# A recurrent layer's time loop: value and beta from one selection product, temporaries in PSUM, 64 steps a turn

## The reference, cut to what matters

```python
def step(S, inp):
    ...
    kn = k_t / (jnp.linalg.norm(k_t, axis=-1, keepdims=True) + 1e-06)
    retrieved = jnp.einsum('bnij,bnj->bni', S, kn)
    delta = v_t - retrieved
    outer = delta[..., :, None] * kn[..., None, :]
    S_upd = jnp.tanh(beta_t[..., None] * S + outer)
    S_new = (1.0 - w) * S + w * S_upd
    Sq = jnp.einsum('bnij,bj->bni', S_new, q_t)
```

## Time and profile before

| | us |
|---|---|
| median of three runs | 9550.41 |
| lowest and highest of them | 9549.36, 9557.72 |
| the profiled execution | 9542.88 |
| its span, first to last instruction | 9541.1 |
| TensorE matmul busy | 7287.1 (76%) |
| TensorE weight loads busy | 4453.7 (47%) |
| VectorE busy | 6764.2 (71%) |
| ScalarE busy | 3257.0 (34%) |
| POOL busy | 3224.7 (34%) |
| mean granted TensorE clock | 0.853 |

### The profile page before, as it was taken

The page is one execution under the profiler, slowest core; times in us unless marked ns, Lnnn a source line. Parts: engine busy times, 40 slices in busy tenths (PEclk is TensorE's granted clock), DMA queues, the critical chain, the costliest instruction groups (busy, mean ns, idle before and its releaser), DMA issues. The chain is left out here.

```text
span 9541.1 us, 245537 instructions
## 1 busy us (share of the span) xinstructions
PE 7287.1 (76%) x92569; PEld 4453.7 (47%) x92569; DVE 6764.2 (71%) x15000; ACT 3257.0 (34%) x5970; POOL 3224.7 (34%) x3982
## 2 busy tenths in 40 slices
PE   4888888888874826656845768888888888888887
PEld 3666666666621212223223345545455545454554
DVE  7777777777758475765485557777777777777776
ACT  2222222222243313223413334444444444444444
POOL 1333333333300000210040035555555555555553
PEclk7888888888887867656865779999999999999999
DMA  0000000000000000000000031111111111111111
GB/s 18 1 1 1 1 1 1 1 1 1 1 5 1 15 0 0 0 0 1 0 0 1 1 120 54 53 53 54 48 56 51 54 51 51 56 51 56 51 56 57
DMA packets 156976, 243.21 MB, mean 25 GB/s; under 512 B 21617, under 2 KB 136849, under 8 KB 150161
## 3 DMA queue, kind: packets, MB, share of 16 engines
q1 hardware_dynamic: 155920, 228.84, 7.8%
HBM read 187.06 MB, written 13.66 MB: 21 GB/s over the span
## 5 line engine op out<-in xcount | busy, mean ns | idle before, releaser
L2751 POOL TENSOR_TENSOR big<-big 128x512 f32<-128x512 f32 x776 | 1040.1, 1373 | 278.4 <-DMA big<-norms 270.7
L2741 POOL TENSOR_TENSOR big<-big 128x512 f32<-128x512 f32 x388 | 494.7, 1275 | 1819.8 <-DVE big L2583 1819.8
L882 POOL TENSOR_TENSOR big<-big 128x128 f32<-128x128 f32 x1024 | 518.3, 506 | 1569.7 <-DVE big L820 1567.4
L604 ACT ACTIVATE big<-big 128x128 f32<-128x128 f32 x1024 | 316.8, 309 | 1902.0 <-DVE big L778 1876.8
L1856 POOL TENSOR_TENSOR small<-big 128x480 f32<-128x480 f32 (+14 forms) x240 | 220.9, 954 | 2187.2 <-ACT big L1614 1866.5
L2158 PE MATMUL banks<-hidden,big 128*128 128x256 f32 x3104 | 828.9, 401 | 111.8 <-DVE big L2583 41.1
L514 PE MATMUL banks<-big,constants_on_chip 128*128 128x128 f32 x2048 | 533.3, 347 | 409.8 <-DVE big L811 408.2
L337 PE MATMUL banks<-big,constants_on_chip 128*128 128x512 f32 (+15 forms) x1088 | 533.5, 644 | 355.2 <-DVE big L1747 191.3
L337 PE MATMUL banks<-big,weights_even 128*128 128x512 f32 (+5 forms) x1152 | 620.5, 692 | 235.0 <-DVE big L1137 45.1
L2222 PE MATMUL banks<-big,hidden 128*32 128x512 f32 x6144 | 770.5, 600 | 4.1 <-ACT big L2473 4.1
L2201 PEld LDWEIGHTS banks<-big 32*32 32x32 f32 x49152 | 535.2, 103 | 471.8 <-issue 471.1
(11 more groups left out here) (349 smaller groups left out, 15896.3 us busy)
## 6 DMA issues: line engine op xcount, KB each, us to landing
big<-norms SPq DMA_DIRECT2D x776, 128.0 KB, 2.9
big<-qk SPq DMA_DIRECT2D x50, 512.0 KB, 4.8
big<-vo SPq DMA_DIRECT2D x25, 1024.0 KB, 5.8
weights_odd<-ffn SPq DMA_DIRECT2D x25, 537.5 KB, 4.6
hidden<-big SPq DMA_DIRECT2D x171, 64.0 KB, 12.9
hidden<-big SPq DMA_DIRECT2D x25, 256.0 KB, 3.8
hidden<-big SPq DMA_DIRECT2D x25, 255.8 KB, 4.0
big<-pairs SPq DMA_DIRECT2D x6, 1024.0 KB, 10.4
```

Of the source, the lines that this page charges most:

```text
L882: nc.gpsimd.tensor_tensor(full(u["kS"][s % 2]), full(S), by(u["ko_c"]), ALU.mult).then_inc(*e.did(("kS", s)))
L2741: self.nc.gpsimd.tensor_tensor(dst, cos, sin, ALU.add).then_inc(*e.did(("turned_pair", f, name, g)))
L2751: self.nc.gpsimd.tensor_tensor(x, x, u["norms"][:, n, g].unsqueeze(1).broadcast_to([P, 2, QTOK]), ALU.mult).then_inc(*e.did(("scaled", f, ...
```

## The change

- A turn holds 64 steps in place of 32, so there are 16 turns.
- Ahead of the loop v and beta of all tokens are computed (`all_tokens`: 128 products of 32 rows by 128 columns each for v and for beta) and kept in SBUF. `xrep`, `repeat_x`, `values`, `logits` and the sigmoids of the loop are gone, and `knext`, the shifted copy of the keys, too.
- In the loop one product per step, `value_and_beta`, takes v(s) and beta(s) out of a 128 x 256 tile of 32 steps (`vb`) with a selection matrix (`own`, the identity repeated); v lands in columns 0 to 127 and beta in columns 128 to 255 of the step's bank (banks 0 and 1 in turn).
- outer and wT are in PSUM bank 2, arg and T in bank 3. bS reads beta from the step's bank.
- TensorE waits for bS(s) ahead of the kS product of delta(s), besides kS and kT; VectorE waits for v(s+1) ahead of bS.
- The small copies for the next 32 steps, and the copies of v and beta, are on ScalarE behind the tanh; VectorE keeps two small instructions per half turn.
- The bf16 product that nobody reads stays, and writes bank 5.

```diff
-STEPS = 32
-PARTS = 1
+STEPS = 64
...
+        own=b[6].rearrange("p (s c) -> p s c", c=P),
...
+        step_bank=core.bank[0:2], outer=core.bank[2][:, 0:128], wT=core.bank[2][:, 128:256],
+        arg=core.bank[3][:, 0:128], T=core.bank[3][:, 128:256], out_bank=[core.bank[4], core.bank[7]],
...
+    def all_tokens(bank, weight, g, start):
+
+        for m in range(4):
+            for b in range(BATCH):
+                at = b * SEQ + (4 * g + m) * HALF_STEPS
+                mm = nc.tensor.matmul(bank[32 * b:32 * b + 32, m * P:(m + 1) * P], u["xp"][:, at:at + HALF_STEPS], weight,
+                                      start=start, stop=True, skip_group_check=True)
+        return mm
...
+    def value_and_beta(s, label):
+
+        nc.tensor.matmul(u["step_bank"][s % 2][:, 0:2 * P], u["own"][:, s % HALF_STEPS, :], u["vb"][s // HALF_STEPS], start=True, stop=False, skip_group_check=True).then_inc(*e.did(label))
...
+    with e.turns("time", CELL_TURNS):
         for s in range(STEPS):
...
+            before, back = (s - 1) % STEPS, {} if s else {"back": 1}
+            bank = u["step_bank"][s % 2][:, 0:P]
+            pe.wait_ge(*e.after("kS", before, **back))
+            pe.wait_ge(*e.after("bS", s, **back))
+            nc.tensor.matmul(bank, core.c("negblock32"), u["kS"][before % 2], start=False, stop=False, skip_group_check=True)
+            pe.wait_ge(*e.after("kT", before, **back))
+            nc.tensor.matmul(bank, core.c("negblock32"), u["kT"], start=False, stop=True,
+                             skip_group_check=True).then_inc(*e.did(("delta", s)))
+            pe.wait_ge(*e.after("S", before, **back))
...
+            read_out(before, ("Sq", before))
+            pe.wait_ge(*e.after("outer", before, **back))
...
+            value_and_beta((s + 1) % STEPS, ("v", (s + 1) % STEPS))
+            nc.tensor.matmul(core.bank[5][:, 0:2 * P], core.half[:, 0:P], core.half[:, 0:2 * P], start=True, stop=True,
                              skip_group_check=True)
...
+            act.wait_ge(*e.after("arg", s))
+            nc.scalar.activation(u["T"], u["arg"], ACT.Tanh).then_inc(*e.did(("T", s)))
...
+            if chore == 2:
+                copy_steps("w_c", "wt", h, start, ("w_c", h))
...
+            if chore == 8:
+                copy_tile("beta", h, start * BATCH, ("vb", h))
...
+            dve.wait_ge(*e.after("delta", s))
+            tt(cut(u["outer"]), cut(u["step_bank"][s % 2][:, 0:P]), spread(u["kn_c"], s), ALU.mult).then_inc(
+                *e.did(("outer", s)))
+            dve.wait_ge(*e.after("outer", s))
+            tt(u["arg"], u["outer"], u["bS"], ALU.add).then_inc(*e.did(("arg", s)))
+            half, chore = 0 if s >= HALF_STEPS else 1, s % HALF_STEPS
+            if chore == 4:
+                dve.wait_ge(*e.after("w_c", half))
+                rest_of_weight(half, ("om_c", half))
+            if chore == 5:
+                dve.wait_ge(*e.after("knext_c", half))
+                weigh_next_key(half)
+            dve.wait_ge(*e.after("T", s))
+            tt(cut(u["kT"]), cut(u["T"]), spread(u["kw_c"], s), ALU.mult).then_inc(*e.did(("kT", s)))
+            tt(cut(u["wT"]), cut(u["T"]), spread(u["w_c"], s), ALU.mult).then_inc(*e.did(("wT", s)))
+            dve.wait_ge(*e.after("aS", s))
...
+            dve.wait_ge(*e.after("wT", s))
+            tt(new, u["wT"], u["aS"], ALU.add).then_inc(*e.did(("S", s)))
+            dve.wait_ge(*e.after("v", ahead))
+            dve.wait_ge(*e.after("S", s))
+            tt(u["bS"], new, u["step_bank"][ahead % 2][:, P:2 * P], ALU.mult).then_inc(*e.did(("bS", ahead)))
```

More of the change, by code:

```diff
@@ L412, in cells_buffers @@
     b = core.b
-    st = core.b[7]
-    cut = lambda a, n: st[:, a:a + n]
+    cut = lambda a, n: b[7][:, a:a + n]
+    by_step = lambda a: cut(a, BLK * STEPS).rearrange("p (n s) -> p n s", n=BLK)
     return dict(
[L416 to L424, removed]
+        xp=b[0], kn=b[1], wt=b[2], v=b[3], qd=b[4], lg=b[5], ex=b[6], tmp=b[7], sq=b[8], beta=b[5],
+        own=b[6].rearrange("p (s c) -> p s c", c=P),
+        S=[cut(0, 128), cut(128, 128)], aS=cut(256, 128), bS=cut(384, 128), kT=cut(512, 128),
+        kS=[cut(640, 128), cut(768, 128)], qd_c=cut(896, BATCH * STEPS), vb=[cut(1152, 256), cut(1408, 256)],
+        kn_c=by_step(2048), w_c=by_step(2304), om_c=by_step(2560), knext_c=by_step(2816), kw_c=by_step(3072),
+        ko_c=by_step(3328),
+        step_bank=core.bank[0:2], outer=core.bank[2][:, 0:128], wT=core.bank[2][:, 128:256],
+        arg=core.bank[3][:, 0:128], T=core.bank[3][:, 128:256], out_bank=[core.bank[4], core.bank[7]],
     )
@@ L462, in cells_tensor @@
         core.product(e, core.to_act, [(core.c("block32"), u["tmp"][:, tok(t)])])
[L464 to L482, removed]
@@ L485, in cells_tensor @@
[L485 to L488, removed]
-        if g >= 2:
[L490 to L496, removed]
+    for k in range(core.to_act.filled - 4, core.to_act.filled):
+        pe.wait_ge(*e.after("drained", "to_act", core.to_act.phase, k))
@@ new lines, in all_tokens @@
+    def all_tokens(bank, weight, g, start):
[5 more added lines that the diff above has]
+        return mm
+    for g in range(TILES):
+        if g >= 2:
+            pe.wait_ge(*e.after("v_kept", g - 2))
+        all_tokens(core.bank[g % 2], w("wv"), g, True).then_inc(*e.did(("v_all", g)))
@@ new lines, in cells_tensor @@
+    for g in range(TILES):
+        if g >= 2:
+            pe.wait_ge(*e.after("beta_kept", g - 2))
+        bank = core.bank[2 + g % 2]
+        nc.tensor.matmul(bank, core.half[:, TILE:TILE + P], core.half[:, 0:TILE], start=True, stop=False,
+                         skip_group_check=True)
+        all_tokens(bank, w("wbeta"), g, False).then_inc(*e.did(("beta_all", g)))
+    def value_and_beta(s, label):
+        nc.tensor.matmul(u["step_bank"][s % 2][:, 0:2 * P], u["own"][:, s % HALF_STEPS, :], u["vb"][s // HALF_STEPS], start=True, stop=False, skip_group_check=True).then_inc(*e.did(label))
@@ L502, in read_out @@
                          start=True, stop=True, skip_group_check=True).then_inc(*e.did(label))
-    with e.turns("time", SEQ // STEPS):
-        for s in range(STEPS):
[L507 to L520, removed]
+    pe.wait_ge(*e.after("vb_first"))
+    pe.wait_ge(*e.after("own"))
+    pe.wait_ge(*e.after("coefficients"))
+    value_and_beta(0, "v_first")
+    with e.turns("time", CELL_TURNS):
+        for s in range(STEPS):
+            before, back = (s - 1) % STEPS, {} if s else {"back": 1}
[7 more added lines that the diff above has]
+            pe.wait_ge(*e.after("S", before, **back))
             if s == 1:
@@ L526, in cells_tensor @@
                 pe.wait_ge(*e.after("out", 1))
[L527 to L543, removed]
+            read_out(before, ("Sq", before))
+            pe.wait_ge(*e.after("outer", before, **back))
+            if s + 1 == HALF_STEPS:
+                pe.wait_ge(*e.after("vb", 1))
+            if s + 1 == STEPS:
+                pe.wait_ge(*e.after("vb", 0))
+            value_and_beta((s + 1) % STEPS, ("v", (s + 1) % STEPS))
+            nc.tensor.matmul(core.bank[5][:, 0:2 * P], core.half[:, 0:P], core.half[:, 0:2 * P], start=True, stop=True,
                              skip_group_check=True)
-    pe.wait_ge(*e.after("S", STEPS - 1, PARTS - 1))
+    pe.wait_ge(*e.after("S", STEPS - 1))
     read_out(STEPS - 1, "Sq_last")
-    for label in [("beta", G - 1), ("out_last",)]:
-        pe.wait_ge(*e.after(*label))
+    pe.wait_ge(*e.after("bS", 0))
+    pe.wait_ge(*e.after("out_last"))
     for t in range(TILES):
@@ L579, in cells_scalar @@
         core.found.at[("cells", "knorm", t)] = core.found.at[("cells", *label)]
+    for g in range(TILES):
+        act.wait_ge(*e.after("v_all", g))
+        nc.scalar.activation(u["v"][:, tok(g)], core.bank[g % 2], ACT.Copy).then_inc(*e.did(("v_kept", g)))
     act.wait_ge(*e.after("lmax"))
     nc.scalar.activation(u["ex"][:, 0:TOK], u["lg"][:, 0:TOK], ACT.Exp).then_inc(*e.did("lexp"))
-    act.wait_ge(*e.after("staged"))
[L585 to L596, removed]
+    for g in range(TILES):
+        act.wait_ge(*e.after("beta_all", g))
+        if g == 0:
+            act.wait_ge(*e.after("lexp"))
+        nc.scalar.activation(u["beta"][:, tok(g)], core.bank[2 + g % 2], ACT.Sigmoid).then_inc(*e.did(("beta_kept", g)))
@@ new lines, in cells_scalar, with copy, copy_steps, copy_tile @@
+    act.wait_ge(*e.after("staged"))
+    def copy(dst, src, label=None):
+        nc.scalar.activation(dst, src, ACT.Copy).then_inc(*e.did(label))
+    def copy_steps(dst, name, h, start, label):
+        last = {"knext_c": 1}.get(dst, 0)
+        src = u[name][:, last:TOK + last].rearrange("p (n t) -> p n t", n=BLK)
+        copy(u[dst][:, :, half_steps(h)], src[:, :, bass.ds(start, HALF_STEPS)], label)
+    def copy_tile(name, h, start, label):
+        at = {"v": 0, "beta": P}[name]
+        copy(u["vb"][h][:, at:at + P], u[name][:, bass.ds(start, P)], label)
@@ new lines, in keep_out @@
```

(35 more changed lines are left out.)

137 lines of the change are left out of this document (33 added, 104 removed).

## The result

The changed kernel takes 10585.19 us (median of 4 runs, 10582.71 to 10600.62) against 9554.06 for the kernel before: ratio 1.108, 95% interval 1.106 to 1.110, 1031 us slower. The forecast was slower, 10390 us, 10060 to 10680. The profiled execution takes 10583.84 us, its span is 10582.1.

What follows compares the result with a forecast made beforehand. VectorE's ring of dependent instructions was taken to bound the time loop, 2.30 us a step. Loop +850 and start -9 gave +841 on 9542.88, so 10384, and 10390 as median; range 10060 to 10680 us.

Steps and rivals of the forecast that it cites:

- The edit that decides: In the time loop, TensorE's wait for bS puts its delta work behind VectorE's last instructions: +0.89 us a step.
- The temporaries: Loop temporaries in PSUM: arg 0.26 us and tanh 0.03 us shorter a step, other VectorE instructions unchanged.
- rival 3: PSUM operands are dear: five VectorE instructions in the loop each a fifth longer, 299 us, total 10690; chance 0.07.
- The clock: Loop's granted clock falls from 0.87 to 0.70, six tenths of the time low: +0.31 us a step, 313 us.
- rival 2: The clock is low throughout the loop: 522 us in place of 313, total 10600; chance 0.18.
- own range: Whole kernel: 10290 to 10500 us, the main forecast with 0.1 us a step of PSUM to either side.
- the wider one: Whole kernel: 10060 to 10680 us, adding the always-high and always-low clock cases with their PSUM bounds.
- Loop and turns: Time loop: 1024 steps of 2.91 us plus clock, turns (28 us) and chores, 3327 us against 2477: +850.
- the chores: Small VectorE copies in the loop: 64 stay, mostly covered by the tanh, 6 us; the others move to ScalarE free.
- Ahead of the loop: Products for v and beta run where TensorE idles; the loop starts near 155 us in place of 164.4: -9 us.
- Every later layer keeping its length: Behind the time loop: a sign to look for, every later stage unchanged in length.

Runs made afterwards that it cites:

- experiment 2: Kernel before plus one line: TensorE waits for bS(s) ahead of kS in delta(s), nothing else changed; 10700.43 us in a single execution.
- experiment 1: Changed kernel with beta selected into its own PSUM bank by a second product, wait for bS removed; 9246.78 us, ratio 0.965 to the kernel before.
- experiment 4: Changed kernel with the unused bf16 product four times, twice or not at all per step: 10192.73, 10705.82, 10691.62 us; experiment 1's kernel without it: 9271.51 us.
- experiment 5: Changed kernel without the unused product: 10696.22 us; the same with 64 small products ahead of the loop: 10595.97; changed kernel with those 64 only: 10696.60.

## Why the prediction was right, and where it was off

**The edit that decides: right.** +0.89 us at the high clock and 1.32 us behind bS at the low one were forecast; the steps are 2.91 us (four unused products) and 3.42 us (the change), to the 0.01 of the sum. TensorE's wait is for bS, as said; experiment 2 adds it by itself, and experiment 1 removes it together with what makes it needless, a bank and a product for beta.

**The temporaries: sum right, reason wrong.** The tanh went to 262 ns in place of 309 (I had 278, for reading a bank only). The -0.26 us of arg was booked first to arg's PSUM input, though the prediction also saw that POOL's aS would be done before the later arg. In the changed kernel the second reason suffices: the gain comes without PSUM (experiment 2) and stays when the temporaries leave (291 ns). It does belong to PSUM where the wait is gone. VectorE's instructions from and to PSUM take 286 to 299 ns, so rival 3 fell. The 62 cycles of "VectorE: DVE Perf Modes" in the Trainium skill (section on the TRN2 errata) are not seen in these rows.

**The clock: the term that was mis-sized.** I took six tenths of the time at the low level, midway between two rows by busy share. It was all of it, rival 2: 0.4 x 0.51 x 1024 = 209 us more, and the result stands 195 above the forecast. The busy share was the wrong basis: TensorE is busy 79% of the new loop, not the 55 to 60% that rival 2 expected, and at the low level all the same, and experiment 4 has 85% at 0.50 and 62% at 0.99. No variant of this loop showed a value midway. The forecast's own range, 10290 to 10500, does not hold the result; the wider one holds it through rival 2, which had a chance of 0.18. The ends of that wider range are not worked out as they are described: 10078 less 0.1 us a step would be 9976, and 10600 more it 10702.

**Loop and turns.** 15 turns and the chores came to about 33 us (3535 less 1024 x 3.42) where I had 34, but by terms that offset each other. The turns took 24 us in place of 28. In every turn four other steps are longer, by 0.11, 0.11, 0.21 and 0.21 us, 10 us in the whole loop; only one of them holds a small VectorE instruction (0.11 us), so the chores cost under 2 us in place of 6, and the rest has no cause on record. **Ahead of the loop** 155.5 was forecast as 155; the 256 products for v and beta ended at 94 us and delayed nothing. Every later layer keeping its length held here: the ninth took 3689 us against 3694 before. The prediction did not weigh that moved code can change it, so by experiment 5 that was luck.

## What to carry to other kernels

When a kernel guards a PSUM bank that two engines share with a wait, price that wait before sharing. Here it cost the two products that stand between the wait and what the bounding engine needs, 0.80 us a step at the high clock and 1.32 at the low one, though TensorE's other products stayed hidden. A bank of its own for the second thing was cheaper, even with one more product a step. No run here shows whether the shared bank would work without the wait. When such a wait is added, look at the granted clock too: in experiment 2 the loop went from 0.87 to 0.50 with it, and the low level alone was worth 500 us. So price both levels, and not a mix by busy share. When a change moves code, compare the layers that it does not touch before crediting the difference to the edit.

## What the runs showed that I had not expected

The granted clock of the loop was 0.50 in every kernel that waits for bS but the one with four unused products (0.99); only in experiment 2 were its first 7 us at the high level. The kernels that do not wait had 0.85 to 0.95. Taking 128 TensorE instructions out ahead of an untouched 3.7 ms layer, or putting 128 in, made it 104 to 125 us longer, 1% of the run, in each of the four profiled executions of such kernels; in experiment 1's kernel taking them out made 10 us.
